# A two-layer mixer on one core: another order of VectorE's, GpSimd's and TensorE's work in the first pair of tiles

## The reference

```python
xn = layernorm(x)
s = silu(einsum('bsh,ih->bsi', xn, w_gate))                 # 1376 values per token
_, idx = top_k(-abs(s), 688)                                # the 688 smallest magnitudes
s = s.at[rows, idx].set(0.0)                                # are set to zero
s = einsum('bsi,hi->bsh', s * einsum('bsh,ih->bsi', xn, w_up), w_down)
thresh = 0.7 * mean(abs(weight), axis=-1)                   # per row of the ternary weight
q = where(weight > thresh, 1, where(weight < -thresh, -1, 0))
g = silu(einsum('bsd,od->bso', xn, q) + bias)
x1 = x + s * g
```

## Time and profile before

| What | Value |
|---|---|
| median of 3 runs | 631.98 us (630.73 to 631.99) |
| span of the profiled execution, first to last instruction | 629.6 us |
| its own time | not given; the runs lie 1.1 to 2.4 us above its span |
| TensorE busy (matmuls) | 593.6 us, 94% |
| VectorE busy | 487.0 us, 77% |
| ScalarE busy | 339.8 us, 54% |
| GpSimd busy | 188.7 us, 30% |

### The profile page before, as it was taken

The page is one execution under the profiler, slowest core; times in us unless marked ns, Lnnn a source line. Parts: engine busy times, 40 slices in busy tenths (PEclk is TensorE's granted clock), DMA queues, the critical chain, the costliest instruction groups (busy, mean ns, idle before and its releaser), DMA issues. The chain is left out here.

```text
span 629.6 us, 8823 instructions
## 1 busy us (share of the span) xinstructions
PE 593.6 (94%) x2852; PEld 461.9 (73%) x2852; DVE 487.0 (77%) x940; ACT 339.8 (54%) x571; POOL 188.7 (30%) x303
## 2 busy tenths in 40 slices
PE   8969999999999999999999999999798999999775
PEld 6857888787888888888888888886575665656432
DVE  6998889888788789788878878768576676666556
ACT  6848567347428626744842862685463544455420
POOL 2332002001000200100100020079985666663344
PEclk9979999999999999999999999999979999999887
DMA  8801000020030020011003001091030000000015
GB/s 348 320 21 41 27 2 1 25 77 2 1 100 0 0 100 0 0 34 66 0 0 100 0 1 68 1 333 44 3 68 1 0 1 1 1 2 1 1 67 200
DMA packets 17194, 32.35 MB, mean 51 GB/s; under 512 B 3238, under 2 KB 3750, under 8 KB 17164
## 3 DMA queue, kind: packets, MB, share of 16 engines
q1 hardware_dynamic: 17164, 31.99, 14.6%
HBM read 24.63 MB, written 7.35 MB: 51 GB/s over the span
## 5 line engine op out<-in xcount | busy, mean ns | idle before, releaser
L857 DVE TENSOR_SCALAR_CACHE_REDUCE junk_d<-k_buf,cand 128x1376 int8<-128x1376 f32 x56 | 91.9, 1640 | 0.3
L650 ACT ACTIVATE junk_a<-k_buf,cand 128x1376 int8<-128x1376 f32 x56 | 80.5, 1437 | 0.6
L1197 PE MATMUL ps_a<-wd_hi,zt_hi 128*128 128x512 f32 (+1 forms) x176 | 71.9, 409 | 0.2 <-DVE zt_lo L976 0.2
L629 ACT ACTIVATE s_buf<-ps_a 128x1376 f32<-128x1376 f32 x16 | 21.1, 1318 | 94.0 <-PE ps_a L1164 89.4
L1197 PE MATMUL ps_a<-wd_hi,zt_lo 128*128 128x512 f32 (+1 forms) x176 | 69.2, 393 | 0.0
L1197 PE MATMUL ps_a<-wd_lo,zt_hi 128*128 128x512 f32 (+1 forms) x176 | 68.9, 391 | 0.0
L527 POOL TENSOR_TENSOR xres<-xres,gate 128x512 f32<-128x512 f32 x12 | 22.3, 1860 | 130.8 <-DVE gate L983 130.8
L519 POOL TENSOR_TENSOR rstd<-var_eps,expo 128x2 f32<-128x2 f32 x7 | 4.9, 703 | 164.9 <-DVE var_eps L779 164.9
L1164 PE MATMUL ps_b<-wu_hi,xt_hi 128*128 128x512 f32 (+1 forms) x192 | 52.4, 381 | 0.0
L1164 PE MATMUL ps_a<-wg_hi,xt_hi 128*128 128x512 f32 (+1 forms) x192 | 51.9, 379 | 0.0
L1164 PE MATMUL ps_a<-wg_lo,xt_hi 128*128 128x512 f32 (+1 forms) x192 | 50.8, 373 | 1.1 <-DVE wg_lo L762 1.1
(11 more groups left out here) (249 smaller groups left out, 1378.8 us busy)
## 6 DMA issues: line engine op xcount, KB each, us to landing
xres<-in_x SPq DMA_DIRECT2D x8, 512.0 KB, 3.3
out<-arena SPq DMA_DIRECT2D x16, 256.0 KB, 2.0
xin<-in_x SPq DMA_DIRECT2D x7, 512.0 KB, 3.9
x_scratch<-xres SPq DMA_DIRECT2D x6, 514.0 KB, 3.8
arena<-x_scratch SPq DMA_DIRECT2D x3, 1028.0 KB, 12.4
m_buf<-in_wg_t SPq DMA_DIRECT2D x2, 688.0 KB, 5.0
k_buf<-in_wg_t SPq DMA_DIRECT2D x2, 688.0 KB, 7.9
m_buf<-in_wu_t SPq DMA_DIRECT2D x2, 688.0 KB, 7.6
```

What stands on the lines that cost most here:

```text
L629: act.activation(s_buf[:, t, :], ps_a[:].rearrange("p a n -> p (a n)")[:, 0:INNER], ACT.Silu).then_inc(s_ready, 1)
L650: act.activation(junk_a[:], k_buf[:, 1, :], ACT.Sign, bias=c, scale=-1.0, accum_out=below[:, 1:2]).then_inc(act_step, 1)
L857: dve.tensor_scalar(junk_d[:], k_buf[:, 0, :], c, -float(DROP), ALU.is_lt, ALU.add, accum_out=e).then_inc(cnt_dve, 1)
L1197: last = pe.matmul(ps_a[:, t, :], zs, ws[0:rows, c, :], start=(c == 0 and n == 0), stop=(c == CHUNKS - 1 and n == 2))
```

## The change

- `down_low` can work on one 512-column half of a unit, with one step of `wd_l` for each. GpSimd does units 8 and 9 in halves, then `root(1)`, then units 10, 11 and 12 in halves, each half behind a wait for `candlow_ready`, which VectorE raises at the start of the halvings 1 to 6, then unit 13 without such a wait. All counts of `wd_l` elsewhere follow (`lows_through`, `N_LOW` = 11).
- The scratch of `ternary_values` is a bank of `ps_t` in PSUM instead of `gate2` in SBUF.
- VectorE: product of tile 0 ahead of the thresholds and values; the statistics of pair 1 ahead of halve 1, `norm_apply` behind it.
- ScalarE: `tern_copy` 0 and 1 behind silu and keys of tile 1; `split_hi` of unit 13 after search 3 instead of 4; `at_most_first` after search 4 instead of 5.
- TensorE: the up projection of tile 1 directly behind the gate projection of tile 1, with `tern_transpose` 0 and 1 ahead of its second block of rows and 2 and 3 ahead of its fourth.

```diff
@@ block_a @@
+            def lows_through(u):
+                return sum(units[v][4] or 1 for v in range(N_GU, u + 1))
+            N_LOW = lows_through(len(units) - 1)
@@ sync: loads @@
-                            sp.wait_ge(wd_l, prev[-1] - N_GU + 1)
+                            sp.wait_ge(wd_l, lows_through(prev[-1]))
...
-                        sp.wait_ge(wd_l, len(units) - N_GU)
+                        sp.wait_ge(wd_l, N_LOW)
@@ gpsimd @@
-                def down_low(u):
+                def down_low(u, j=None):
+                    low, staged, high = units[u][3], slot_ap(u), units[u][2]
+                    if j is not None:
+                        low, staged, high = low[:, j, :], staged[:, j, :], high[:, j, :]
                     pool.wait_ge(w_hi, u + 1)
-                    pool.tensor_tensor(units[u][3], slot_ap(u), units[u][2].bitcast(F32),
-                                       ALU.subtract).then_inc(wd_l, 1)
+                    pool.tensor_tensor(low, staged, high.bitcast(F32), ALU.subtract).then_inc(wd_l, 1)
+                def beside_count(n):
+                    pool.wait_ge(candlow_ready, n)
...
-                for u in range(N_GU, N_GU + 4):
-                    down_low(u)
+                for u in range(N_GU, N_GU + 2):
+                    for j in range(2):
+                        down_low(u, j)
                 root(1)
-                for u in range(N_GU + 4, len(units)):
-                    down_low(u)
+                for u in range(N_GU + 2, N_GU + 4):
+                    for j in range(2):
+                        beside_count(2 * (u - N_GU - 2) + j + 1)
+                        down_low(u, j)
+                for j in range(2):
+                    beside_count(5 + j)
+                    down_low(N_GU + 4, j)
+                down_low(N_GU + 5)
@@ scalar: silu_keys, pair @@
-                        act.wait_ge(wd_l, 2)
+                        act.wait_ge(wd_l, lows_through(N_GU + 1))
...
-                            for k in range(2):
-                                tern_copy(k)
+                    if first:
+                        for k in range(2):
+                            tern_copy(k)
                     search_start(p)
...
-                            if n in (1, 4):
-                                split_hi(N_GU + 4 + n // 4)
-                            if n == 5:
+                            if n in (1, 3):
+                                split_hi(N_GU + 4 + n // 3)
+                            if n == 4:
                                 at_most_first(p)
@@ vector: ternary_values, first_pair @@
-                    neg = gate2[:, k % 2, :]
+                    neg = ps_t[:, k % 2, :]
...
                     halve(0, 0)
+                    product(0, 0)
                     ternary_thresholds()
                     for k in range(KH):
                         ternary_values(k)
-                    product(0, 0)
+                    norm_stats(1)
                     halve(0, 1)
+                    norm_apply(1)
                     halve(0, 2)
-                    norm_stats(1)
                     halve(0, 3)
-                    norm_apply(1)
                     product(0, 1)
...
-                    dve.wait_ge(wd_l, len(units) - N_GU)
+                    dve.wait_ge(wd_l, N_LOW)
@@ tensor: project, down, first_pair @@
-                        if k == at and between is not None:
+                        if isinstance(between, dict):
+                            if k in between:
+                                between[k]()
+                        elif k == at and between is not None:
                             between()
...
-                        pe.wait_ge(wd_l, len(units) - N_GU)
+                        pe.wait_ge(wd_l, N_LOW)
...
                     gate_project(0, 1)
-                    tern_transpose(0)
-                    tern_transpose(1)
-                    up_project(0, 1, lambda: [tern_transpose(k) for k in range(2, KH)])
+                    up_project(0, 1, {1: lambda: [tern_transpose(k) for k in range(2)],
+                                      3: lambda: [tern_transpose(k) for k in range(2, KH)]})
```

## The result

The changed kernel takes 626.02 us (median of 4 runs, 624.77 to 627.67) against 631.68 us (4 runs, 630.73 to 631.99): ratio 0.9908, 95% interval [0.9885, 0.9931], 5.7 us less. The forecast was 625.7. The profiled execution took 626.69 us, with a span of 624.9 against 629.6 before. TensorE is busy for 592.0 us of it (95%).

What follows compares the result with a forecast made beforehand. TensorE was taken to bound from 80 us, so the gain is its earlier gapless start, held back by VectorE contending with GpSimd: 7.0 at the product, 6.25 at the flag; 629.6 - 6.3 = 623.3 span, plus 2.4 gives 625.7, range 623.6 to 628.5.

Steps and rivals of the forecast that it cites:

- a fall of the clock between 42 and 48 us: Sign of being wrong: TensorE's granted clock falling in that window, around the ternary matmuls, in the changed profile.
- Contention as the cause of the 12.98 us: Four ternary blocks on VectorE: 4.8 us undisturbed, 8.2 us from taking turns with GpSimd.
- Thresholds: Two 128x4 VectorE instructions, now behind GpSimd's start, each wait for a piece: 2.34 us instead of 0.41.
- The rival in which they slip through: Small threshold instructions pass between GpSimd's pieces, TensorE binds tile 1's product: gain 7.9, 624.1 us; chance 0.15.
- Values: Ternary values with scratch in PSUM no longer wait for GpSimd: 5.6 us, bounds 4.8 to 8.1, done at 34.1.
- The rival in which PSUM does not free VectorE: Ternary values still wait for GpSimd's two remaining pieces: 2.5 us back, 628.2 us; chance 0.12.
- Product of tile 1: VectorE, not TensorE, sets its start at 43.2 us instead of 50.16, a gain of 7.0 there.
- the rival in which the time rose to 632.9: VectorE's counts hold what GpSimd needs, so pieces delay `rise` 1.25 us six times: 7.2 us, slower; chance 0.05.
- From the product to the flag: Tile 1's product to tile 0's selection: 11.34 - 0.2 + 0.9 = 12.04 us, cutting the gain to 6.25.
- The collision of the last unit with `rise`: GpSimd's last unit follows unit 12's second piece into count 6's step and delays `rise`: 0.9 us, bounds zero to 1.3.
- The clock before the ternary matmuls: Rival: TensorE idle from about 42.5 to 44.9, clock falls to 1.2 GHz, matmuls 1.9 us longer: 627.6 us; chance 0.06.
- Loss further on: Rival: the gain is lost later to a wait that does not move: no change, 631.5 us; chance 0.03.

Runs made afterwards that it cites:

- the change's second repeat: The unmodified changed kernel run a third time, on one chip beside three other kernels; 626.46 us, ratio 0.9901 to the kernel before.
- the first set: Changed kernel again, 626.44 us, beside the changed kernel with 20 idle transposes on TensorE ahead of the ternary matmuls, 626.49 us.
- the third: On one chip: changed kernel again, 626.46 us, beside the changed kernel with 20 idle transposes ahead of the ternary matmuls, 625.36 us.
- the runs with the gap filled: Changed kernel plus 20 idle transposes in TensorE's gap between pair 1's x transposes and the ternary matmuls, run twice; 626.49 and 625.36 us.

## Why the prediction was right, and where it was off

**The total** came out right: 626.02 against 625.7, the sign with it. The time is 1.8 us over the span in every execution of the change; the 2.4 that the prediction added held 0.6 by which the profiled execution of the kernel before lay under its median. That the hit is so close is in part luck: this 0.6 made up for what the clock cost the median. The span was forecast at 623.3; the profiled execution took 624.9, two others 623.5 and 623.0. And one of the prediction's own signs of being wrong did appear in the profile, a fall of the clock between 42 and 48 us.

**Contention as the cause of the 12.98 us.** Shown. One line that takes away the second SBUF input (or the SBUF target) brings the values to 5.80 us beside GpSimd's units whole and in their old places, and F−G from 42.87 to 36.16.

**Thresholds.** Right: 1.22 us for the second where 1.3 was forecast, values from 28.45 where 28.5 was. The rival in which they slip through is out in every profile with 512-column pieces, and the run with the thresholds first shows what the wait costs: 1.6 to 1.8 us at P.

**Values.** Within the bounds, 0.2 us over the sum: an `is_lt` into PSUM takes 0.75 (taken: 0.69), the subtraction 0.75 as before. By the Trainium skill, "VectorE: DVE Perf Modes", section "Why PSUM operands drop a tier", the estimate was 0.27 more than in SBUF; the trace agrees, 0.75 less 0.49. The rival in which PSUM does not free VectorE is out: beside GpSimd's third and fourth piece the first pair of values takes 0.76 and 0.75 with the scratch in PSUM, 1.47 and 1.67 with it in SBUF.

**Product of tile 1.** Forecast 43.2, measured 43.45 with G 0.23 later (24.66 against 24.43), released by VectorE's own order as said.

**Counts.** 1.64 to 1.65 in all steps with a piece inside; the rival in which the time rose to 632.9 is out.

**From the product to the flag.** The sum gave 17.14 + 0.7 = 17.84; where the clock holds it is 17.74 (the change's second repeat, both runs with the gap filled). The collision of the last unit with `rise` cost 0.88 (1.04 less 0.16) against 0.9. In that repeat the flag matmul came at 61.11, forecast 61.05, after 0.78 of waiting, forecast 1.

**The clock before the ternary matmuls** is the step that was mis-sized. The prediction gave it 0.06, because the fall of before came over four us into a hole. That row shows one hole and one fall; it does not bound from below how short a hole can be. In three profiled executions of the change, all with gaps of 2.21 to 2.23 us, the clock fell in two; with the scratch in SBUF it held at 2.23. There F−P is 19.14 and 19.28, 1.4 and 1.5 us over 17.74; the price forecast was 1.9. So the profiled execution went by that rival and its flag came 1.54 later than forecast, 1.40 of it this. On the median the effect is smaller and not settled: none in the first set, 1.1 us in the third, where differences of 1.6 us in the second layer lie on top. The median mixes executions with and without a fall, so the forecast of 625.7, made for the case without one, could come close to it; the runs with the gap filled took 625.36 and 626.49.

**Loss further on.** Out: from the gate projection at 67.69 to the second layer's first transposes the change takes 385.00 us, the kernel before 384.91, and no run leaves 384.4 to 385.5. The rest of the kernel takes 171.7 to 174.0 us, in the three profiles of the change 171.7, 172.2 and 173.3; that is why the medians follow F−G only to about 1 us.

**What the prediction did not ask** was which of its edits carry the gain. In the old order the scratch alone is worth 7.4 us. In the new orders neither cure (scratch in SBUF, whole units) gives 631.78 us, the scratch in PSUM alone 627.02, the held-back pieces alone 626.31, both together 626.02 to 626.46. Scratch and pieces are two cures for one contention: either gives most of the gain, the second adds 1 us at most (between medians of different chips), and the orders without them give nearly nothing. It is only the new order that pays for its thresholds (1.6 to 1.8 us), and the change's gain could be had for one line. The pieces in the old order were not tried.

## What to carry to other kernels

When VectorE and GpSimd take turns, look first at where VectorE's operands lie: a scratch in PSUM made eight 512-column instructions immune for 0.26 us each on four of them, without touching any order. Before moving work to where GpSimd runs, look at the smallest instructions that move with it: a 4-column one waits for up to a whole GpSimd instruction, so place it ahead of GpSimd's start, and let GpSimd's pieces start with a long VectorE instruction that doesn't contend. When a long hole of TensorE is closed, look for the shorter one that takes its place, and price the clock's fall there even if the trace of before shows none at that length.

## What the runs showed of the hardware

- The granted clock fell from 2.4 to 1.2 GHz at a gap of TensorE of 2.2 us in some executions and not in others of the same program (2.21 us in the change, with a fall, and in its second repeat, without). It need not fall inside the gap: it fell 0.3 us after the matmuls had resumed in the change, and 1.3 us after they had resumed from a gap of 2.64 in the run with whole units. It also fell in the profiles with gaps of 3.14 and 5.56 us, and no profile with the gap at 1.04 or less had a fall there.
- GpSimd is slowed as well: its 1024-column subtraction took 2.95 and 2.58 us where the 512-column values contended with it and 2.42 where they did not. Beside the waiting 4-column thresholds it lost nothing (2.40 and 2.42 in the run with the orders only).
- A contending VectorE instruction waits for what is left of GpSimd's, however small it is itself: 128x4 took 2.08 and 2.33 us beside 1024-column units and 0.80 and 1.22 beside 512-column pieces; alone it takes 0.17.
